# Involution stage: tiles applied in halves, with the eight pieces of the next band matrix built between the halves

## What is computed

```python
red = jnp.einsum('bchw,oc->bohw', x, w_reduce) + b_reduce[None, :, None, None]
ker = jnp.einsum('bohw,ko->bkhw', red, w_span) + b_span[None, :, None, None]
ker = ker.reshape(B, G, K * K, H, W)                 # 8 groups of channels, 49 taps
xp = jnp.pad(x, ((0, 0), (0, 0), (PAD, PAD), (PAD, PAD)))
patches = jnp.stack([xp[:, :, i * DIL:i * DIL + H, j * DIL:j * DIL + W] for i in range(K) for j in range(K)], axis=2)
patches = patches.reshape(B, G, Cg, K * K, H, W)
out = jnp.einsum('bgckhw,bgkhw->bgchw', patches, ker)
```

## Time and profile before

| | |
|---|---|
| runs | 2849.27, 2830.85, 2848.44 us; median 2848.44 |
| the profiled execution | 2834.71 us, its span 2832.9 us |
| mean granted TensorE clock | 0.907 of full speed |
| the involution stage in the span | 207 to 557 us |
| TensorE busy over the span | 2358.3 us (83%) |
| VectorE, ScalarE, GpSimd busy | 1495.8, 1309.7, 366.5 us |

### The profile page before, as it was taken

How to read it: one execution, slowest core, us unless ns; L and a number is a source line. 1 busy time by engine, 2 the same in 40 slices (tenths; PEclk the granted TensorE clock), 3 DMA queues, 4 the chain that set the end, 5 groups by cost and what they waited for, 6 DMA issues and landing times. The chain is left out here.

```text
span 2832.9 us, 78733 instructions
## 1 busy us (share of the span) xinstructions
PE 2358.3 (83%) x34528; PEld 1799.9 (64%) x34528; DVE 1495.8 (53%) x3482; ACT 1309.7 (46%) x2623; POOL 366.5 (13%) x651
## 2 busy tenths in 40 slices
PE   3549898768169999999999999999785984799898
PEld 2328898633058888888888888888433751344444
DVE  3852433357136665666566566656211452576777
ACT  3443433356046655665566565656210563333332
POOL 1311111124300000000000000000021001122211
PEclk7676977879689999999999999999897886899999
DMA  6457535365621111111101111110398410000000
GB/s 196 144 138 162 107 82 102 73 216 177 153 77 45 45 45 45 45 45 45 36 23 44 45 45 45 45 23 19 123 298 290 140 55 13 13 20 25 21 24 26
DMA packets 155227, 235.09 MB, mean 83 GB/s; under 512 B 18310, under 2 KB 112623, under 8 KB 151372
## 3 DMA queue, kind: packets, MB, share of 16 engines
q1 hardware_dynamic: 122392, 134.74, 16.4%
q0 software_dynamic: 32496, 95.33, 12.5%
HBM read 141.68 MB, written 88.31 MB: 81 GB/s over the span
## 5 line engine op out<-in xcount | busy, mean ns | idle before, releaser
L1026 DVE COPY spc_g<-spc_pz 128x512 f32<-128x512 f32 x1024 | 629.1, 682 | 306.5 <-PE spc_pz L922 306.5
L996 ACT ACTIVATE spc_g<-spc_pz 128x512 f32<-128x512 f32 x1024 | 549.2, 612 | 284.5 <-PE spc_pz L922 284.1
L922 PE MATMUL spc_pz<-spc_v,spc_as 108*128 108x128 bf16 x8192 | 553.9, 219 | 13.8 <-issue 1.7
L922 PEld LDWEIGHTS spc_pz<-spc_v,spc_as 108*128 108x128 bf16 x8192 | 473.6, 97 | 102.7 <-ACT spc_g L996 31.4
L943 PE MATMUL spc_pz<-spc_g,spc_u 128*20 128x128 f32 x16384 | 469.2, 274 | 21.4 <-DVE spc_g L1026 17.3
L943 PEld LDWEIGHTS spc_pz<-spc_g,spc_u 128*20 128x20 f32 x16384 | 451.4, 134 | 47.5 <-ACT spc_g L996 30.1
L1533 PE MATMUL moe_ex<-moe_ew,moe_d 128*128 128x512 f32 x512 | 249.8, 611 | 32.8 <-DVE moe_yt L1690 32.4
L907 PE MATMUL spc_pu<-spc_f,spc_s 128*128 128x256 f32 x768 | 207.6, 396 | 80.6 <-DMA spc_s<-s_sf 80.6
L1690 DVE SCALAR_TENSOR_TENSOR moe_yt<-moe_ex,moe_gb,moe_yt 128x128 f32<-128x128 f32 x768 | 209.6, 343 | 103.3 <-ACT moe_yt L1592 98.0
L566 DVE SCALAR_TENSOR_TENSOR inv_xo<-inv_pa,inv_mask,inv_xo 128x256 f32<-128x256 f32 x256 | 123.6, 484 | 219.7 <-PE inv_pa L524 187.0
L544 ACT ACTIVATE inv_b<-inv_pb 112x1024 f32<-112x1024 f32 x128 | 125.5, 1021 | 216.8 <-PE inv_pb L503 216.8
(11 more groups left out here) (218 smaller groups left out, 2282.0 us busy)
## 6 DMA issues: line engine op xcount, KB each, us to landing
s_yd<-spc_yo SPq DMA_DIRECT2D x128, 160.0 KB
s_sf<-fwd_so SPq DMA_DIRECT2D x16, 1024.0 KB, 6.4
spc_s<-s_sf POOLq DMA_DIRECT2D x32, 512.0 KB, 6.1
ivs_y<-s_yd POOLq DMA_DIRECT2D x32, 512.0 KB, 5.1
s_td<-ivs_to SPq DMA_DIRECT2D x32, 512.0 KB, 5.3
ln_t<-s_td SPq DMA_DIRECT2D x32, 512.0 KB, 3.9
lnc_xc<-in_x SPq DMA_DIRECT2D x32, 256.0 KB, 5.3
s_xn<-lnc_xn SPq DMA_DIRECT2D x64, 128.0 KB
```

Of the source, the lines that this page charges most:

```text
L922: m = pe.matmul(pz[:, (p + 2) % 3, e // 4, 2 * FT * (e % 4):2 * FT * (e % 4) + 2 * FT], AS[:, x, 8 * p + e, :], V[:, k, x, :, FT * t:FT * ...
L996: act.activation(g_out(p, 0), g_in(p, 0), ACT.Copy).then_inc(ga, 1)
L1026: v.tensor_copy(g_out(p, 1), g_in(p, 1)).then_inc(gd, 1)
```

## The change

Each tile is applied in two halves of two images each. `apply_b` gets a third argument: the waits stay ahead of the first half, and `applied` is raised after the second. The eight pieces of the next B are made between the halves: two after the first half of the phase, one after each of the next six, none after the last. The number of instructions and all data stay the same.

```diff
-            def apply_b(n, tw):
+            def apply_b(n, tw, half):
                 s, q = divmod(n, 2)
                 k = (4 * n + tw) % 2
-                if tw == 0:
-                    pe.wait_ge(b_ready, 8 * n + 8)
-                if q == 0:
-                    for band in range(2):
-                        pe.wait_ge(x_in[band][tw], 32 + 32 * s)
-                if 4 * n + tw >= 2:
-                    pe.wait_ge(chosen, 4 * (4 * n + tw - 1))
-                for b in range(NB):
+                if half == 0:
+                    if tw == 0:
+                        pe.wait_ge(b_ready, 8 * n + 8)
+                    if q == 0:
+                        for band in range(2):
+                            pe.wait_ge(x_in[band][tw], 32 + 32 * s)
+                    if 4 * n + tw >= 2:
+                        pe.wait_ge(chosen, 4 * (4 * n + tw - 1))
+                for b in range(2 * half, 2 * half + 2):
...
-                m.then_inc(applied, 1)
+                if half:
+                    m.then_inc(applied, 1)
 
             for p in range(8):
                 make_b(0, p)
             for n in range(NPH):
-                for tw in range(4):
-                    apply_b(n, tw)
+                for i in range(8):
+                    apply_b(n, i // 2, i % 2)
                     if n + 1 < NPH:
-                        make_b(n + 1, 2 * tw)
-                        make_b(n + 1, 2 * tw + 1)
+                        if i == 0:
+                            make_b(n + 1, 0)
+                        if i < 7:
+                            make_b(n + 1, i + 1)
```

## The result

The changed kernel takes 2958.44 us (median of 4, 2926.00 to 2969.64) against 2842.19 (median of 4, 2830.85 to 2849.27): ratio 1.040, 95% interval 1.035 to 1.045. I had forecast 2850, no change, and a range up to 2892. The profiled execution took 2954.62 us, 119.9 more than the profiled one of before.

The account below looks back on a forecast made before the run. TensorE was taken as the bound, its speed depending on the granted clock. This execution's 2834.7 us + 1 direct + 17 for the clock gave 2853; forecast 2850 us, no change, range 2808 to 2892.

Parts of the forecast that it names:

- What goes and what comes: Phase ends lose about 1.0 us of copy wait, -15 us; three more pairs of kind changes a phase add +16.
- the bound of 0.48 us a pair: Upper bound for a pair of changes between apply and make, read at low clock; direct sum then up to +7.
- Rival 3: Changes of kind cost nothing and only the wait goes: -15, so 2836 us with the same clock sum; chance 0.05.
- Moved transfers: Row loads and stores go out later in the phase, but stay covered with 3 us to spare.
- How the clock comes back: Only unbroken apply work raises the clock: one place per phase, not four; a miss costs a phase, 13.6 us lost.
- How often it comes back: Low clock in the stage after the change: 54 us against 37 before, so +17 us.
- three long stretches are 41 us: Two longest issue stalls and one more near 2 us each drop the clock for long, before 13.6 for a missed phase end.
- My reading of the stalls of before: Of seven phases that load rows of X, five show an issue stall of over 1 us.
- Rival 2: Stalls drop the clock in or after every loading phase, halves keep it down to phase end: +58, 2893 us; chance 0.20.
- rival 1: The clock stays up, issue stalls shrink and the wait goes: 2794 us, by half 2815; chance 0.20.
- The tell-tales: Right: full-clock phase 17.0 to 17.1 us, copy wait about 0.2. Wrong: 14 phases at mean clock over 0.95 or under 0.75.
- Low clock lasts in stretches of nearly a phase: Sign that the forecast is right: such low stretches in the stage, ending at a phase's seam.

Follow-up runs that it names:

- e2_last: The kernel before with only the last tile of each phase cut in two, its two pieces between the halves: 2794.93 us, ratio 0.980.
- e5_332: Whole tiles with three, three and two pieces between them, the next phase's first tile right behind the last; edit to the changed kernel: 2809.06 us, ratio 0.991.
- e1_pairs: The changed kernel with both pieces between a tile's halves, so second half and next tile's first half run together: 2833.3 us, ratio 0.996.
- e3_twice: The changed kernel with the last piece of each phase made twice, eight more matmuls: 2884.3 us.
- e9_half: The changed kernel with half of the last piece's matmuls issued twice in each phase: 2878.17 us, ratio to before 1.014.
- e7_after_noload: The changed kernel without the loads of new rows of X in odd phases and without waiting for them: 2864.99 us.
- e10_last_again: Repeat measurement of the kernel before with only each phase's last tile cut in two, pieces between the halves: 2797.07 us, ratio 0.987.

## Why the prediction was wrong, point by point

- **What goes and what comes.** Right. I had -15 and +16 us, 0.35 us for a pair of changes and 0.2 us of wait left. Measured: 0.33, 0.27, and 0.03 to 0.04 us a phase, about +0.6 us in all. Both gaps came from subtracting starts in the earlier trace rows. The 3.41 us of a tile at low clock, in the bound of 0.48 us a pair, stood in none of the rows; the low phase above gives it (3.61 us for the two halves from 441.48, 1.90 for one, so 1.71 a half without a change, 3.42 a tile). Rival 3, changes for nothing, falls. The Trainium skill has, in "TensorEngine Tiling (Array Packing)", Key Properties, that changing the tiling mode drains TensorE; the traces agree in that a change of kind costs time, 0.33 us a pair, and no run shows that it is a drain. That the gain is given back by these changes was true of the direct sum, and was a reason to expect nothing, not a loss.
- **Moved transfers.** Right: after the first phase TensorE never waited on X, and the later loads did not bind.
- **How the clock comes back.** The mechanism was right: half tiles between makes don't raise it, four places became one, and a miss costs a phase (30.62 us against 30.7). Runs with no place, one and two show it: 3004.6, 2958.4 and 2824.1 us. Above that the count doesn't order the times: three places gave 2795 and 2809 us (e2_last, e5_332), four 2833.3 (e1_pairs) and 2842 (before). That e1_pairs does not lead goes with its issue stalls, 19.1 us against 10.7 in the second profile of e2_last; no run tried it.
- **How often it comes back: the step that failed.** The term of the sum that was mis-sized is the low clock after the change. I wrote "three long stretches are 41 us, and one of the three missing its next phase end too, 13.6 more: 54". I took each seam for a draw of its own, with about two chances in three. The profile after showed one fall after the start, and ten seams in a row that missed. Over the same 14 phases as in my sum, 256.47 to 655.82, the low clock took 399.35 - 14 x 17.07 - 1.0 = 159.4 us against the 54 (over the whole stage it is 173.3 against 48.6 before). Nor did the fall come where I had put it: the stall was in the third piece of a phase, not in the last half tile. My reading of the stalls of before was off as well: four, not five, are over 1 us.
- **Why the seams missed together** is not fully shown. A low phase has no waits in it and repeats to the hundredth (30.62 us, ten times). If the clock is set at moments of its own, a seam that misses is followed by one that lies at almost the same place against them. That is my assumption; e3_twice and e9_half, with other phase lengths, took 74 and 80 us off and fit it. The repetition does not lock for good: phases of the same 30.62 us recovered after one miss at the start of this trace (287.09) and after two in e7_after_noload (257.65 and 288.27 missed, 318.89 did not).
- **Which stalls count.** Rival 2 had "stalls go on and drop the clock in or after every loading phase": its direction and its second half (the halves keep the clock down) were the result, at 0.20. Its first half was not: there was one fall, not seven. Its price, seven phases, assumed that the odd phases recover. Fifteen phases are the ceiling, 15 x 13.6 = 204 us, and it belonged in the range: 2834.7 + 1 + 204 - 37 = 3003. The condition of rival 1 half came true: the stalls shrank, to one of 0.95 us, but that one came just ahead of the fall.
- **The tell-tales** mostly worked: a full-clock phase at 17.07, the copy's wait near 0.3 (0.27 in e7_after_noload), and 14 phases at mean clock under 0.75, for rival 2: they had 0.55. "Low clock lasts in stretches of nearly a phase" did not come.

## What to carry to other kernels

Where the granted clock moves within a stage, ask of an edit not only what it removes but where in the new order the clock can come back; a wait removed is worth microseconds and a lost place of recovery may be worth phases. Don't treat repeated phases as independent draws: a steady loop without waits can miss the same way many times in a row, so let the range reach to "always low". And fill a wait with the smallest cut that does it: cutting only the last tile gave 2795 us, cutting all of them 2958.

## What the runs showed that I had not expected

TensorE stood at 1.2 GHz for 319.4 us with no idle time in them, busy with pieces and half tiles. The Trainium skill, "TensorE: Matmul & The Clock Gate", in its section on loop structure, has matmuls that follow each other directly stay warm; this trace does not agree, in that matmuls of 33 rows by 112 columns mixed with short runs of 112 by 64, without a gap, did not become warm again; e7_after_noload agrees in that the same mix, once at full clock, stayed there for 211 us.

More work made the kernel faster: four float32 matmuls more in a phase took 80 us off. And the clock was lost behind an issue stall of only 0.95 us, with a gap of 0.63 us five microseconds before, while in e10_last_again it outlasted stalls of up to 1.95 us. The Trainium skill's "Runtime: NRT & Kernel Launch", Instruction fetch mechanics, calls the fetch mostly hidden. No view says that the issue stalls are the fetch; if they are, then without the row loads the traces agree (no issue wait of the matmuls in the stage), and with them they don't (10.3 us before, 19.1 in e1_pairs).
